# A stencil step, a two-fold normalisation and a mixture of experts in float32: the front reordered, loads packed, work moved to GpSimd

## The reference

```python
Af = A_grid[None] * f[:, None]
Bf = B_grid[None] * f[:, None]
gradv_Af = _grad(Af[:, 0], 1) + _grad(Af[:, 1], 2)
gradvv_Bf = _grad2(Bf[:, 0], 1) + _grad2(Bf[:, 1], 2) + _grad(_grad(Bf[:, 2], 2), 1) + _grad(_grad(Bf[:, 2], 1), 2)
x = jnp.maximum(f + (-gradv_Af + gradvv_Bf * 0.5) * dt[:, None, None], 0.0)
...
h = (x - mu) * jax.lax.rsqrt(var + 1e-05) * ln_g + ln_b      # over features
h_norm = (h - m_t) * jax.lax.rsqrt(v_t + 1e-08)              # over tokens
se = subj_emb[subject_ids]
hyp = jax.nn.relu(se @ hyp_w1 + hyp_b1) @ hyp_w2 + hyp_b2
sty = jax.nn.relu(hyp @ sty_w1 + sty_b1) @ sty_w2 + sty_b2
gamma, beta = jnp.split(sty, 2, axis=-1)
h = h_norm * (jax.nn.softplus(gamma) + 1e-08)[:, None, :] + beta[:, None, :]
probs = softmax(h_flat @ router_w)   # top 2 of 8, normalised: combine
hid = jax.nn.relu(jnp.einsum('nd,edf->nef', h_flat, exp_w1) + exp_b1)
eout = jnp.einsum('nef,efd->ned', hid, exp_w2) + exp_b2
y = x + jnp.einsum('ned,ne->nd', eout, combine)
```

## Time and profile before

| | us |
|---|---|
| Median of 3 runs | 119.53 (119.53 to 120.2) |
| Span of the profiled execution | 117.9 |
| Own time of the profiled execution | not listed; two of the three runs show 119.53 |
| TensorE, weight loads | 111.9 (95%), 85.0 (72%) |
| VectorE | 91.8 (78%) |
| ScalarE | 75.5 (64%) |
| GpSimd | 8.8 (7%) |

### The profile page before, as it was taken

How to read it: one execution, slowest core, us unless ns; L and a number is a source line. 1 busy time by engine, 2 the same in 40 slices (tenths; PEclk the granted TensorE clock), 3 DMA queues, 4 the chain that set the end, 5 groups by cost and what they waited for, 6 DMA issues and landing times.

```text
span 117.9 us, 1519 instructions
## 1 busy us (share of the span) xinstructions
PE 111.9 (95%) x506; PEld 85.0 (72%) x506; DVE 91.8 (78%) x198; ACT 75.5 (64%) x99; POOL 8.8 (7%) x18
## 2 busy tenths in 40 slices
PE   6999999998999999999999999999999999999960
PEld 2469894446646688888888888888888888888850
DVE  0398789748993496999959976996799589879781
ACT  0403456756361997777777777777777777777800
POOL 1437430000000000000000000000000000000040
PEclk9999999999999999999999999999999999999998
DMA  2999991000000270050400040021004000500004
GB/s 94 310 366 418 407 407 47 0 0 0 0 0 6 96 266 0 8 178 0 178 0 0 29 152 0 0 120 64 0 0 178 0 0 8 170 0 6 0 0 178
DMA packets 4583, 10.86 MB, mean 92 GB/s; under 512 B 800, under 2 KB 1888, under 8 KB 4576
## 3 DMA queue, kind: packets, MB, share of 16 engines
q1 hardware_dynamic: 3920, 9.93, 22.4%
q10 hardware_dynamic: 656, 0.84, 2.3%
HBM read 10.21 MB, written 0.56 MB: 91 GB/s over the span
## 4 chain that ended last, share of the span: by engine, by line
PE 84%; DVE 7%; DMA 4%; issue 1%; ACT 1%; SPq 0%; DVEq 0%
PE zt L625 11%; PE zt L626 11%; PE zt L627 11%; PE zt L614 6%; PE aux L653 6%; PE aux L650 6%; PE aux L649 6%; PE yt L653 5%; PE yt L650 5%; PE yt L649 5%; PE yt L619 4%; DMA gn<-in_grids_dram 4%; DVE st L824 2%; DVE h L853 1%; PE aux L574 1%; PE zt L543 1%
## 5 line engine op out<-in xcount | busy, mean ns | idle before, releaser
L498 ACT ACTIVATE hid_hi<-zt,pv 128x1024 fp32r<-128x1024 f32 x27 | 30.2, 1120 | 17.4 <-PE zt L627 17.3
L945 DVE TENSOR_TENSOR hid_lo<-hid,hid_hi 128x1024 fp32r<-128x1024 f32 x27 | 33.0, 1221 | 10.0 <-issue 5.4
L503 ACT ACTIVATE hid<-zt,pv 128x1024 f32<-128x1024 f32 x27 | 29.9, 1108 | 0.0
L625 PE MATMUL zt<-h_hi,ws 128*128 128x512 f32 x56 | 22.7, 406 | 0.0
L626 PE MATMUL zt<-h_hi,ws 128*128 128x512 f32 x56 | 21.8, 390 | 0.0
L627 PE MATMUL zt<-h_lo,ws 128*128 128x512 f32 x56 | 21.8, 389 | 0.0
L625 PEld LDWEIGHTS zt<-h_hi,ws 128*128 128x128 f32 x56 | 10.5, 188 | 3.0 <-issue 0.5
L626 PEld LDWEIGHTS zt<-h_hi,ws 128*128 128x128 f32 x56 | 10.5, 188 | 2.5 <-issue 0.5
L627 PEld LDWEIGHTS zt<-h_lo,ws 128*128 128x128 f32 x56 | 10.5, 188 | 2.2
L650 PE MATMUL aux<-hid_hi,ws 128*128 128x512 f32 (+1 forms) x32 | 12.0, 376 | 0.0
L649 PE MATMUL aux<-hid_hi,ws 128*128 128x512 f32 (+1 forms) x32 | 12.0, 376 | 0.0
(11 more groups left out here) (136 smaller groups left out, 143.0 us busy)
## 6 DMA issues: line engine op xcount, KB each, us to landing
we<-in_exp_w_dram SPq DMA_DIRECT2D x8, 512.0 KB, 9.1
gate_all<-gates_dram SPq DMA_DIRECT2D x8, 512.0 KB, 3.5
f<-in_x_dram SPq DMA_DIRECT2D x2, 256.0 KB, 4.5
ft<-in_x_exchanged_dram ACTq DMA_DIRECT2D x2, 256.0 KB, 5.3
out_dram<-acc SPq DMA_DIRECT2D x1, 256.0 KB, 2.1
out_dram<-acc SPq DMA_DIRECT2D x2, 128.0 KB, 2.0
first<-d_difference_dt_ids_dram ACTq DMA_DIRECT2D x1, 136.0 KB, 3.2
gn<-in_grids_dram SPq DMA_DIRECT2D x1, 128.0 KB, 4.4
```

What stands on the lines that cost most here:

```text
L498: act.activation(hid_hi[:, c, :], zt[c % 2][:], ACT.Relu, bias=bias).then_inc(hi_ready, 1)
L503: act.activation(hid[:, c, :], zt[c % 2][:], ACT.Relu, bias=bias).then_inc(hid_ready, 1)
L625: pe.matmul(zt[c % 2][:, tok], w_hi, h_hi[:, tok], start=True, stop=False)
L945: v.tensor_tensor(hid_lo[:, c, :], hid[:, c, :], hid_hi[:, c, :].bitcast(F32), ALU.subtract).then_inc(lo_ready, 1)
```

## The change

Loads: `first` also holds the a0 and b0 grids; `second` holds the b1 and a1 grids and `neg_half_diff2` in one load. `pv` is loaded ahead of the second half of `f`, and the second half of `ft` goes to the SP queue, ahead of the weights. The identity isn't loaded; GpSimd makes it by an iota and a comparison with zero, as its first work.

Steps: `s_b2` of the first half is made in two pieces; the second half's `u_a0` goes to GpSimd, which now makes `u_a1`, `u_a0`, `u_b1`, `u_b0` in this order. The two `gsq` operations stand before `s_b2` of the second half. Relus of a half's last pair are issued one by one. Statistics are aggregated pair by pair; the root over tokens is taken from `mv2` itself, with scale and bias; both Newton chains multiply the mean, gamma or `tg` beside the square instead of after it. Net layers 0 and 1 stand ahead of `columns_b(0)` and `columns_w(0)`. The second half's products have another order, in which `rows_b(1)` is last. One `layer2_0` product moves behind `norm_transposed(1)`. `keep_warm` counts are 7, 1 and 0.

```diff
-WARM_START = 9
-WARM_H = (7, 2)
+WARM_START = 7
+WARM_H = (1, 0)
...
             load(f[:, 0:BH, :], x[:, 0:BH, :], f_in[0])
-            load(gn[:], grids, gn_in)
-            load(gt[:], gridsT, gt_in)
-            load(neg_half_diff2, second_diff, diff2_in)
+            load(second[:], second_operands, second_in)
+            load(pv[:], p128, p128_in)
             load(f[:, BH:B, :], x[:, BH:B, :], f_in[1])
-            load(pv[:], p128, p128_in)
+            load(ft[:, BH:B, :], xT[:, BH:B, :], ft_in[1])
...
+            step(pool.iota(col_minus_row[:], pattern=[[1, P]], base=0, channel_multiplier=-1,
+                           allow_small_or_imprecise_dtypes=True))
+            pool.tensor_scalar(ident, col_minus_row[:], 0.0, None, ALU.is_equal).then_inc(ident_ready, 1)
...
-            pool.wait_ge(s_ready[1], 1)
-            pool.wait_ge(f_in[1], 16)
-            pool.wait_ge(gn_in, 16)
-            product(u_b0, f, gn[:, 1, :]).then_inc(b0_ready[1], 1)
-            pool.wait_ge(ft_in[1], 16)
-            pool.wait_ge(gt_in, 16)
-            product(u_a1, ft, gt[:, 1, :]).then_inc(a1_ready[1], 1)
-            product(u_b1, ft, gt[:, 0, :]).then_inc(b1_ready[1], 1)
+            pool.wait_ge(ft_in[1], 16)
+            pool.wait_ge(second_in, 16)
+            product(u_a1, ft, a1_grid).then_inc(a1_ready[1], 1)
+            pool.wait_ge(f_in[1], 16)
+            product(u_a0, f, a0_grid).then_inc(a0_ready[1], 1)
+            product(u_b1, ft, b1_grid).then_inc(b1_ready[1], 1)
+            product(u_b0, f, b0_grid).then_inc(b0_ready[1], 1)
...
             embedded()
-            relu_step(0)
-            relu_step(2)
             hyper_first()
+            relu_step(0, 2)
+            relu_step(2, 1)
+            relu_step(3, 1)
             hyper_second()
+            style_first()
             inverse_sd_features(0)
-            style_first()
+            style_parts()
             normalise(0)
-            softplus()
+            style_log()
             inverse_sd_tokens(0)
...
-            rows_a(0, start=True)
-            pe.wait_ge(diff2_in, 16)
-            rows_b(0, 0, start=False)
-            rows_b(0, 1, start=False)
-            columns_b(0)
-            columns_w(0, 0, final=True)
-            columns_w(0, 1, final=True)
+            rows_a(0)
+            pe.wait_ge(second_in, 16)
+            rows_b(0, final=False)
             pe.wait_ge(onehot_ready, 1)
             pe.wait_ge(p64_in, 16)
             net_layer(0, pw[0:NS, EMB_AT:EMB_AT + SE], onehot[:], SE)
-            step_cross(1, 0)
+            columns_b(0, 0)
+            columns_b(0, 1)
             net_layer(1, pw[:, HW1_AT:HW1_AT + SH], se[:], SH)
-            step_cross(1, 1)
-            rows_b(1, 0, start=True)
+            columns_w(0, 0, final=True)
+            columns_w(0, 1, final=True)
             pe.wait_ge(p128_in, 16)
             net_layer(2, pv[:, HW2_AT:HW2_AT + SH], hyp1[:], SH)
-            rows_b(1, 1, start=True)
+            step_cross(1, 0)
             net_layer(3, pv[:, SW1_AT:SW1_AT + SE], hyp2[:], SE)
-            columns_w(1, 0, final=False)
+            step_cross(1, 1)
             pe.wait_ge(net_sb, 4)
...
-            columns_w(1, 1, final=False)
-            pe.wait_ge(ident_in, 16)
+            rows_a(1)
+            columns_b(1, 0)
+            pe.wait_ge(ident_ready, 1)
             pe.wait_ge(xp_ready, BH)
             norm_transposed(0)
-            columns_b(1)
+            columns_b(1, 1)
+            columns_w(1, 0, final=False)
+            columns_w(1, 1, final=False)
             step_transposed(0)
-            rows_a(1, start=False)
+            rows_b(1, final=True)
...
             layer2_0(0, 0)
-            layer2_0(0, 1)
             pe.wait_ge(xp_ready, B)
             norm_transposed(1)
+            layer2_0(0, 1)
...
             def scale_and_shift(n, shifted, moved):
                 hb = batches(n)
                 v.wait_ge(rs2_ready, n + 1)
+                squared = mark(v.tensor_tensor(sq2[:, hb], rough2[:, hb], rough2[:, hb], ALU.mult))
                 v.wait_ge(dve, moved)
+                with_t = mark(v.tensor_tensor(rough_t[:, hb], rough2[:, hb], tg[:, hb], ALU.mult))
+                with_g = mark(v.tensor_tensor(rough_g[:, hb], rough2[:, hb], gamma_g[:, hb], ALU.mult))
+                v.wait_ge(dve, squared)
+                then(v.tensor_tensor(vs2[:, hb], ve2[:, hb], sq2[:, hb], ALU.mult))
+                v.wait_ge(dve, with_t)
+                added = mark(v.scalar_tensor_tensor(shift0[:, hb], vs2[:, hb], 3.0, rough_t[:, hb], ALU.subtract, ALU.mult))
```

More of the change, by code:

```diff
@@ L34 @@
 SLOTS = 2
-HALF_DIFF2, IDENT = range(2)
-DIFF_AT = P
-DT_AT = 2 * P
+A0_AT = P
+B0_AT = 2 * P
+DIFF_AT = 3 * P
+DT_AT = 4 * P
 IDS_AT = DT_AT + B
@@ L152, in build @@
         gsum = sb("gsum", [P, B])
-        gamma = sb("gamma", [P, B])
         half_gamma = sb("half_gamma", [P, B])
@@ L202, in build @@
         ident = ident_t[:]
-        neg_half_diff2 = neg_half_diff2_t[:]
+        neg_half_diff2 = second[:, 2, :]
         b2_grid, diff = first[:, 0:P], first[:, DIFF_AT:DIFF_AT + P]
+        a0_grid, b0_grid = first[:, A0_AT:A0_AT + P], first[:, B0_AT:B0_AT + P]
+        b1_grid, a1_grid = second[:, 0, :], second[:, 1, :]
         dtb = first[:, DT_AT:DT_AT + B]
@@ L430, in inverse_sd_tokens @@
             def inverse_sd_tokens(n):
-                act.wait_ge(var2_ready, n + 1)
-                act.activation(lv2[:, batches(n)], ve2[:, batches(n)], ACT.Ln).then_inc(lv2_ready, 1)
+                act.wait_ge(gsq_ready, 1)
+                act.wait_ge(var2_ready, BH * (n + 1))
+                act.activation(lv2[:, batches(n)], mv2[:, batches(n), 1], ACT.Ln, bias=eps_tok[:, 0:1],
+                               scale=gsq[:, 0:1]).then_inc(lv2_ready, 1)
                 act.wait_ge(lv2_ready, n + 1)
@@ L795, in feature_stats @@
             def feature_stats(n):
-                for b in range(n * BH, (n + 1) * BH):
-                    v.wait_ge(xs_ready, b // 2 + 1)
-                    last = mark(v.bn_stats(st1[:, b, :], xs[:, b, :]))
-                v.wait_ge(dve, last)
-                for b in range(n * BH, (n + 1) * BH):
-                    v.bn_aggr(mv1[:, b, :], st1[:, b, :]).then_inc(var1_ready, 1)
-            def refined(n, variance, eps, rough, sq, vs, rs):
+                for k in range(2):
+                    pair = range(n * BH + 2 * k, n * BH + 2 * k + 2)
+                    for b in pair:
+                        v.wait_ge(xs_ready, b + 1 + (b % BH == 0))
+                        last = mark(v.bn_stats(st1[:, b, :], xs[:, b, :]))
+                    v.wait_ge(dve, last)
+                    for b in pair:
+                        v.bn_aggr(mv1[:, b, :], st1[:, b, :]).then_inc(var1_ready, 1)
@@ L821, in token_stats @@
             def token_stats(n):
-                for b in range(n * BH, (n + 1) * BH):
-                    v.wait_ge(xnT_ready, b // 2 + 1)
-                    last = mark(v.bn_stats(st2[:, b, :], own(b)))
-                v.wait_ge(dve, last)
-                for b in range(n * BH, (n + 1) * BH):
-                    last = mark(v.bn_aggr(mv2[:, b, :], st2[:, b, :]))
-                v.wait_ge(dve, last)
-                v.tensor_scalar(ve2[:, batches(n)], mv2[:, batches(n), 1], gsq[:, 0:1], 1e-8, ALU.mult,
-                                ALU.add).then_inc(var2_ready, 1)
@@ L831, in token_stats @@
-                then(v.tensor_scalar(mh[:, batches(n)], mv2[:, batches(n), 0], minus_half_g[:, 0:1], ln_b, ALU.mult,
-                                     ALU.add))
+                for k in range(2):
+                    pair = range(n * BH + 2 * k, n * BH + 2 * k + 2)
+                    for b in pair:
+                        v.wait_ge(xnT_ready, b // 2 + 1)
+                        last = mark(v.bn_stats(st2[:, b, :], own(b)))
+                    v.wait_ge(dve, last)
+                    for b in pair:
+                        v.bn_aggr(mv2[:, b, :], st2[:, b, :]).then_inc(var2_ready, 1)
@@ L833, in token_stats, with token_centre @@
+            def token_centre(n):
+                hb = batches(n)
+                v.wait_ge(var2_ready, BH * (n + 1))
+                shifted = mark(v.tensor_scalar(ve2[:, hb], mv2[:, hb, 1], gsq[:, 0:1], 1e-8, ALU.mult, ALU.add))
+                then(v.tensor_scalar(mh[:, hb], mv2[:, hb, 0], minus_half_g[:, 0:1], ln_b, ALU.mult, ALU.add))
                 v.wait_ge(gamma_ready, 2)
-                return mark(v.scalar_tensor_tensor(tg[:, batches(n)], mh[:, batches(n)], ln_b, half_gamma[:, batches(n)],
-                                                   ALU.subtract, ALU.mult))
@@ L919, in _ @@
             normalise(0)
-            product(u_a0, f, 1, gn[:, 0, :]).then_inc(a0_ready[1], 1)
-            v.wait_ge(dve, squared)
-            moved = token_stats(0)
-            scale_and_shift(0, moved)
+            v.wait_ge(gsq_ready, 2)
+            token_stats(0)
+            parts = token_centre(0)
```

(1 more changed line is left out.)

147 lines of the change are left out of this document (78 added, 69 removed).

## The result

The changed kernel takes 122.55 us (median of 4 runs, 121.5 to 123.36); the kernel before took 119.87 in the same comparison. The ratio is 1.0156, with a 95% interval of 1.0108 to 1.0204, so it is slower, by 1 to 2%; the medians lie 2.2% apart. I had forecast 118.3 us in a range of 117.5 to 119.5, and had given slower by over 1% 4 in 100. The ratios here are not worked out from all runs of a kernel (its slow ones can be left out), so where the times fall into groups I give the groups as well. The profiled run of the changed kernel is the one of 123.36 us.

What follows compares the result with a forecast made beforehand. No single bound: TensorE is busy behind 29.18 us, dependent chains ahead of it set the layer 1 starts. Gains of 0.1 + 0.35 + 0.1 + 0.4 + 0.1 + 0.15 + 0.05 = 1.25 us give 118.3 us, range 117.5 to 119.5.

Steps and rivals of the forecast that it cites:

- The six warm products that go were filler there: TensorE ahead of the first half's layer 1: removing six keep_warm products was taken to cost nothing.
- T0: Start of the first half's expert layer 1: 19.57 us before, forecast 18.37, a gain of 1.2.
- A: The first update neg_xp on VectorE, which waits for TensorE: 9.91 us before, forecast 9.80, bounds 9.6 to 10.3.
- T1: Start of the second half's first expert layer: 29.18 us before, forecast 27.93, a gain of 1.25.
- The clock rival: Seven warm products leave TensorE pausing 0.6 us, its clock rises late, A and T0 come 1.5 us later: 119.8; chance 0.12.
- The landing of `first`: First load, grown from 136 to 264 KB: landing taken at 4.15 us, between 3.95 and 4.65.
- the forecast gain of 0.1: Loads and TensorE's waits less the nets moved ahead: A 0.1 us earlier, 9.80 against 9.91.
- The second rival: Loads land late, first at 4.65 and second and ft at 7 or later: A 10.3, time 118.8; chance 0.2.
- TensorE's start to A: 5.00 us before, less 0.56 for two waits, plus 0.55 for two net layers put ahead: 4.99.
- From A to T0: Statistics, roots, normalisation and h of the first half: from A at 9.80 to T0 at 18.37, through shorter chains and reordering.
- a sign of being wrong in kind: Marks set beforehand: T1 - T0 under 9.2 or over 9.9, or GpSimd's products over 1.4 us.
- T1 - T0: Between the two halves' layer 1 starts: 9.56 us for 9.61, acc copy following TensorE's last transposes, ScalarE's h directly behind it.

Runs made afterwards that it cites:

- split_first: Changed kernel with the a0 and b0 grids again a load of their own, filler still 7, (1, 0): 121.05 us (119.32 to 122.67).
- less_fill: Kernel before with only the changed filler counts, 7, (1, 0) for 9, (7, 2): 121.49 us, ratio 1.0156.
- second2: Changed kernel with only the 2 warm products ahead of the second half's layer 1 put back: 122.03 us, groups at 119.77 to 120.09 and 122.0 to 122.33.
- best_b: best_a with the second half's u_a0 on VectorE again and rows_b(1) ahead of rows_a(1): 120.44 us (119.26 to 122.75).
- start11: Changed kernel with 11 warm products at the start, later counts still 1 and 0: 120.38 us, ratio 1.0067.
- fill_all: Changed kernel with the old filler counts 9, (7, 2): 120.16 us, ratio 1.0025.
- loads_only: Kernel before with only the a0 and b0 grids packed into first and gn not loaded: 120.23 us, ratio 1.0018.
- nets_back: Changed kernel, loads packed, filler 9, (7, 2), all net layers behind the first half's column products: 121.05 us (120.09 to 123.74).
- best_a: Changed kernel with net layers behind the first half's column products, a0 and b0 grids loaded apart, filler 9, (4, 2): 121.01 us.
- best_d: best_a with s_b2 earlier, part of the second half's products between the nets, first root ahead of style_first: 119.74 us, ratio 1.0007.
- best_h: best_d with second-half u_a0 on VectorE, its products behind the transposes, normalise(0) before softplus, warm products between nets, filler 9, (1, 2): 119.3 us, ratio 0.9982.

## Why the prediction was wrong

**The step that failed** is "The six warm products that go were filler there" (and two at the start, two ahead of T1), priced at nothing. I had asked whether a part of the path waits for them (none does in the old kernel: without them T0 - A is 9.65 and T1 - T0 9.61, with them 9.66 and 9.61), not what they do for the clock behind them. Put back alone they are worth 2.4 us in the changed kernel; taken out alone they cost the old one 1.7 (119.77 to 121.49). The other 1.9 us of the miss are the front itself, the terms below.

**The clock rival** had the mechanism and nearly the place: 2.04 us for the first cross products was its mark, and that is the row. Two things were undersized. The chance of 0.12 rested on a TensorE pause of 0.6 us; it was 1.39, since seven products ended at 4.34 and `first` was late. But the length of the pause doesn't decide alone. The trace's first clock record lies at 3.85 to 7.12 us in the 16 profiles with nine or more warm products; in those with seven, whose warm products all ran at the lower level, it lies at 4.15 and 4.71 (`split_first`, `less_fill`) or at 9.07 and 9.87 (changed kernel, `second2`). At the top of the first range is `best_b`, which worked without a pause from 1.17 on and whose first cross products yet took 1.91 us. So the moment at which the clock comes up varies from run to run, and in these four profiles seven products are over, or nearly so, before it; whether it then comes up in the pause is what differs. And the price of 1.5 for the start was 2.2 (`second2`), with a second fall behind T1 that I had no term for: 1.7 us in the profiled run. My argument against it, that a pause of 0.4 us ahead of 29.18 lowered nothing, came from a kernel in which two warm products stood just ahead of it. In the changed one the pause is 0.64, with the 8-column products of L616 on both sides; that it is this stretch is argued from the rows and from `second2`, in which the two products remove the fall. But `start11` made it rare without them, with the same pause, and `less_fill` has a pause of 0.83 us there and no fall in its profiled run, so what exactly decides it stays open. The Trainium skill (TensorE: Matmul & The Clock Gate, Part 1) ties the clock to recent activity; the runs agree in kind.

**The landing of `first`** was the second mis-sized term: 4.15 taken, upper bound 4.65 (by its own sum, 3.95 and 0.37 twice, 4.69). VectorE, which follows it by 0.12, starts at 4.96 to 5.16 where it is 264 KB (`fill_all`, `loads_only`, after), so it landed at 4.84 to 5.04. My bound added bytes at the stretch's rate to 3.2 us; the load took 4.1 to 4.3 (4.7 in `nets_back`). That is 0.7 to 0.9 us on TensorE's start, and alone turns the forecast gain of 0.1 into a loss. My lower end was no better founded: it came from one profile, and VectorE started between 3.86 and 4.94 in the 12 profiles in which `first` is 136 KB, so 4.07 was one of the early ones. The second rival, loads that come late, thus held too, and was undersized too: its A of 10.3 was 10.82 in `fill_all`.

**TensorE's start to A**: 4.99 forecast, 5.28 in `fill_all` (10.82 - 5.54). Without the two waits 4.24 is left, 0.76 less than before where I had 0.56, but 0.76 is also what a late `first` alone takes off (`less_fill`). The rest is 5.28 - 4.24 = 1.04 us. From group to group against `loads_only`, the two net layers take 0.52 of it, as forecast (0.55); the column products between and behind them take 0.30 longer, the first cross products 0.13, and 0.09 is the wait ahead of the one-hot's product. I had the one-hot ready before 7.7; it hangs on `first` and ended at 8.23 (`fill_all`, weight loads):

```profile
8.46 0.19 PEld L542 LDWEIGHTS zt<-onehot,pw 32*64 32x64 f32 x2 [0.33 <-POOL onehot L350]
```

**From A to T0**, forecast 8.57, in the changed kernel 8.98. By its own steps: A to the refinement 3.37 (3.25 forecast), to `xn` 0.65 (0.70), to the statistics 1.02 (0.80: the transposes stand behind `columns_b(1, 0)`, and statistics wait 0.49 for them), to the second root's square 2.20 (2.05, the logarithm with scale and bias 0.39), to `h` 0.96 (0.84), to T0 0.78 (0.92). Six small errors with one sign but two; the direction of all was right, and 0.7 us were gained here.

**GpSimd and VectorE.** I took the rule of the Trainium skill (GPSIMD Engine Reference, section 8, Key points) for a matter of a few tenths of us. The traces bear it out, and the cost is higher: an operation of VectorE with two SBUF inputs that meets a GpSimd product waits until that product ends and then takes roughly its own time, and GpSimd's next product waits for it in turn. In the changed kernel GpSimd's first product ends at 10.26 and `s_b2` at 10.80; the second product, listed from 10.22, ends at 11.93, which is its 1.27 after about 10.7. Its 1.71 us is over the 1.4 that I had called a sign of being wrong in kind. There the collision was hidden by TensorE; in `best_a` it moved A by about 0.9 us, and in `best_d` it put 0.8 on the refinement.

**What held**: identity on GpSimd costs nothing (0.25 and 0.54 us, from 0.82 on); no waits for `gn` and `neg_half_diff` are left; T1 - T0 is 9.48 for 9.56, with the `acc` copy behind TensorE's last transposes and directly ahead of ScalarE's `h`; nothing behind T1 waits for weights. With the filler back the balance of `fill_all` against my T1 of 27.93 is: TensorE's start +0.73 (5.54 for 4.81), from there to A +0.29, A to T0 +0.70 (9.27 for 8.57, 0.3 of it the seven warm products), T1 - T0 -0.23 (9.33 for 9.56); the sum is 1.49, which is 29.42 - 27.93.

**What stays open.** Why the start's clock came up in time in five of twelve runs of `second2` and not in seven; what lowers the clock behind T1 in one run and not in another; whether a `best_h` with fewer warm products in the gaps of the nets is faster still; and by how much `best_h` beats the kernel before, for which 12 runs aren't enough.

## What to carry to other kernels

Ask of each piece of filler what clock the work behind it runs at, not only who waits for it; when an edit moves the start of real work, count the filler anew, and test it by changing the counts alone in the old kernel too. Several kernels here had two groups of times 1.3 to 2 us apart, so one profile or three runs could have told either story; the landing of a first load, too, moved by 1 us between profiles of equal loads. Packing operands into one load removes a wait but delays the first product to the last byte: keep small what the first instruction needs, and keep GpSimd's long products away from the short two-input operations of VectorE that stand on the path.

## What the runs showed of the hardware that I had not expected

- The clock of TensorE can come up late without being listed: in the changed kernel the granted clock reads 1.00 at 5.7 to 9 us, where the trace has no record, while the groups follow each other at 1.83 and 1.61 us instead of 0.96 and 0.87. Equal groups compared from start to start are the surer sign.
- With nine or more warm products the first clock record lies anywhere from 3.85 to 7.12 us, so the same filler is enough in one run and short in another.
- A fall can come behind work that looks dense: PE was busy 2.77 of the 3.41 us ahead of the window at 0.50, but with a 0.64 us pause and eight 8-column products on each side of it. The same stretch in `start11` was followed by no fall.
- VectorE with two SBUF inputs and GpSimd exclude each other for a whole instruction: a `sq` of 128x4 took up to 0.98 us instead of 0.16, `s_b2` 1.30 to 1.79 instead of 0.68, GpSimd's products 1.54 to 1.80 instead of 1.27.
- A bigger first load costs more than its bytes, and equal loads scatter: VectorE started at 3.86 to 4.94 us with 136 KB (12 profiles, middle 4.4) and at 4.96 to 5.48 with 264 KB (8 profiles, middle 5.06). That is 0.66 us for 128 KB, where the stretch's 348 GB/s would make it 0.37.
